# Two loads and two adds moved around the last groups of attention heads, and two transfers swapped in each pair's step

## The reference

```python
Q = Q * cos + _rotate_half(Q) * sin
K = K * cos + _rotate_half(K) * sin
scores = jnp.einsum('bhqd,bhkd->bhqk', Q, K) / scale
scores = jnp.where(causal, scores, jnp.float32(-jnp.inf))
attn = jax.nn.softmax(scores, axis=-1)
out = jnp.einsum('bhqk,bhkd->bhqd', attn, V)
out = out.transpose(0, 2, 1, 3).reshape(B, S, H)
return out @ Wo.T + bo
...
x = x + attention(layernorm(x))
x = x + (silu(xn @ gate_w.T * gate_s) * (xn @ up_w.T * up_s)) @ down_w.T * down_s   # xn = layernorm(x)
```

## Time and profile before

| what | value |
|---|---|
| median of 3 runs | 750.68 us (748.65 to 753.9) |
| the profiled execution | 749.88 us |
| its span, first to last instruction | 748.2 us |
| TensorE busy | 732.0 us, 98% |
| VectorE, ScalarE, GpSimd busy | 443.8, 310.9, 247.7 us |
| TensorE's granted clock | 0.999 |

### The profile page before, as it was taken

The page is one execution under the profiler, slowest core; times in us unless marked ns, Lnnn a source line. Parts: engine busy times, 40 slices in busy tenths (PEclk is TensorE's granted clock), DMA queues, the critical chain, the costliest instruction groups (busy, mean ns, idle before and its releaser), DMA issues.

```text
span 748.2 us, 10633 instructions
## 1 busy us (share of the span) xinstructions
PE 732.0 (98%) x3563; PEld 539.3 (72%) x3563; DVE 443.8 (59%) x1071; ACT 310.9 (42%) x641; POOL 247.7 (33%) x224
## 2 busy tenths in 40 slices
PE   8999999999999999999999999999999999999996
PEld 7887888766656666666666548788788888888885
DVE  6978684897778787777878545853243125114113
ACT  3322231266666666666666662222332232222221
POOL 0816152411114242333324245822232223223223
PEclk9999999999999999999999999999999999999999
DMA  8686469635576667676667356540001001001001
GB/s 280 230 284 232 162 254 309 255 115 160 162 192 172 185 172 194 168 188 164 187 162 187 102 185 225 222 201 1 0 20 38 0 1 56 0 0 56 1 1 59
DMA packets 54318, 104.39 MB, mean 140 GB/s; under 512 B 14820, under 2 KB 18404, under 8 KB 53748
## 3 DMA queue, kind: packets, MB, share of 16 engines
q1 hardware_dynamic: 54264, 103.72, 44.0%
HBM read 69.62 MB, written 38.21 MB: 144 GB/s over the span
## 4 chain that ended last, share of the span: by engine, by line
PE 81%; DVE 6%; issue 5%; DMA 3%; POOL 2%; ACT 1%; SPq 1%; DVEq 0%; POOLq 0%; ACTq 0%
PE ps L1105 32%; PE ps L1244 18%; PE ps L1130 10%; PE ps L1223 10%; PE ps L1320 9%; DMA x_st<-in_x 1%; PE ps L1097 1%; POOL hid_lo L592 1%; DVE xn L786 1%; DVE stats L771 1%; DMA rec_l<-rec_rows 1%; DMA w_st<-in_wk 1%; DMA l_cols<-o_raw 1%; ACT p L683 0%; DVE esin L893 0%
## 5 line engine op out<-in xcount | busy, mean ns | idle before, releaser
L683 ACT ACTIVATE p<-ps 128x384 f32<-128x384 f32 (+3 forms) x384 | 162.0, 489 | 58.0 <-PE ps L1223 57.8
L843 DVE CUSTOM_DVE_ANT_0 masked<-ps,mask_qk 128x512 bf16<-128x512 f32 (+1 forms) x240 | 113.2, 500 | 56.6 <-PE ps L1130 55.7
L1244 PE MATMUL ps<-p,v_slot 128*64 128x512 f32 (+3 forms) x768 | 137.3, 494 | 0.2 <-ACT o_raw L690 0.2
L1223 PE MATMUL ps<-q_st,k_st 99*128 99x384 f32 (+2 forms) x384 | 135.7, 361 | 1.1 <-ACT p L683 1.0
L1056 DVE SCALAR_TENSOR_TENSOR hid<-ps,us_sb,silu 128x512 f32<-128x512 f32 x44 | 33.0, 751 | 165.2 <-PE ps L1105 159.5
L1130 PE MATMUL ps<-k_st,q_st 96*128 96x512 f32 (+2 forms) x384 | 128.9, 357 | 2.0 <-DVE row_max L843 1.7
L592 POOL TENSOR_TENSOR hid_lo<-hid,hid_hi 128x512 fp32r<-128x512 f32 x44 | 56.8, 1290 | 173.0 <-ACT hid_hi L758 173.0
L561 POOL TENSOR_SCALAR_AFFINE_SELECT p<-p 128x512 f32<-128x512 f32 x64 | 40.6, 635 | 209.0 <-ACT p L683 209.0
L1244 PEld LDWEIGHTS ps<-p,v_slot 128*64 128x64 f32 x768 | 50.1, 136 | 74.2 <-issue 62.2
L1130 PEld LDWEIGHTS ps<-k_st,q_st 96*128 96x128 f32 x384 | 72.3, 189 | 29.7 <-DVE row_max L843 14.3
L1223 PEld LDWEIGHTS ps<-q_st,k_st 99*128 99x128 f32 x384 | 72.1, 189 | 16.9 <-issue 6.3
(11 more groups left out here) (117 smaller groups left out, 1080.8 us busy)
## 6 DMA issues: line engine op xcount, KB each, us to landing
qk_scratch<-st_hi SPq DMA_DIRECT2D x32, 512.0 KB, 3.6
q_st<-qk_scratch SPq DMA_DIRECT2D x32, 384.0 KB, 3.8
k_st<-qk_scratch SPq DMA_DIRECT2D x32, 384.0 KB, 4.8
flag_st<-in_ffn SPq DMA_DIRECT2D x32, 264.0 KB, 2.8
ffn_copy<-in_ffn SPq DMA_DIRECT2D x32, 264.0 KB, 3.5
qk_scratch<-st_lo SPq DMA_DIRECT2D x16, 512.0 KB, 3.7
o_T<-o_raw SPq DMA_DIRECT2D x32, 128.0 KB, 4.2
rec_l<-rec_rows SPq DMA_DIRECT2D x32, 128.0 KB, 3.3
```

The source lines that it names most:

```text
L683: act.activation(p32[:, at:at + q0 + w - keep], ps[:, ST_BANK + i % ST_RING, keep - q0:w], ACT.Exp, scale=SCALE).then_inc(exp_done, 1)
L843: ins = dve.tensor_tensor_reduce((masked_a if u < 2 else masked)[:, s_before(i) % 2, col:col + kept], scores, mask_qk[:, 512 - kept:512], ...
L1223: pe.matmul(ps[:, ST_BANK + i % ST_RING, 0:w], k_st[0:K_ALL, slot, kt * P:(kt + 1) * P], q_st[0:K_ALL, slot, q0:q0 + w], start=True, stop= ...
L1244: ins = pe.matmul(ps[VW * a:VW * (a + 1), o_bank(u, half), q0 - 512 * half:512], v_slot[:, slot, kt, :], p32[:, at:at + n], start=(kt == 0 ...
```

## The change

Two things move, and nothing is added or taken away.

In an even step SP's rows of maxima (`load_max(t + 1)`) now come ahead of `move_pair` and `store_rec`, and within `move_pair` the two moves of sums come ahead of the two moves of values.

At the end, the loads of `bo_sb` and `ds_sb` wait for one pair less of weighted values (`pv_half[1]` at 15 instead of 16) and come ahead of `move_pair(14)`; GpSimd does `add_bias(0)` ahead of `scale_group(6)` and `add_bias(1)` ahead of `scale_group(7)`.

```diff
--- before.py
+++ after.py
@@ -427,9 +427,11 @@
                     sp.wait_ge(l_out, 16 * (u // 2))
                 for a in range(2):
                     t = 2 * u + a
+                    sp.dma_start(l_cols[:, t % 4, :], o_raw[2 * D * a + D:2 * D * a + D + 1, u % 2, :].rearrange("o (p e) -> o p e", e=KT)).then_inc(o_moved[u % 2], 16)
+                for a in range(2):
+                    t = 2 * u + a
                     rows = slice(t % 4 * D, (t % 4 + 1) * D)
                     sp.dma_start(o_T[rows, t // 4, :], o_raw[2 * D * a:2 * D * a + D, u % 2, :]).then_inc(o_moved[u % 2], 16)
-                    sp.dma_start(l_cols[:, t % 4, :], o_raw[2 * D * a + D:2 * D * a + D + 1, u % 2, :].rearrange("o (p e) -> o p e", e=KT)).then_inc(o_moved[u % 2], 16)
 
             def store_rec(g):
 
@@ -445,12 +447,12 @@
                     sp.dma_start(rec_l[h * D:(h + 1) * D, :], rec_rows[g, h].partition_broadcast(D)).then_inc(rec_in, 16)
 
             def b_step(t):
+                if t + 1 < HEADS:
+                    load_max(t + 1)
                 if t % 2 == 0 and t >= 4:
                     move_pair((t - 4) // 2)
                 if t % 4 == 3 and t >= 7:
                     store_rec((t - 7) // 4)
-                if t + 1 < HEADS:
-                    load_max(t + 1)
 
                 cols = slice(t * FFN_PIECE, (t + 1) * FFN_PIECE)
                 if t == 0:
@@ -476,10 +478,10 @@
             sp.wait_ge(v_copied, HEADS)
             load_x(xr[:, 0, :, :], 0).then_inc(xr_in[0], 16)
             load_x(xr[:, 1, :, :], 1).then_inc(xr_in[1], 16)
-            move_pair(PAIRS - 2)
-            sp.wait_ge(pv_half[1], PAIRS)
+            sp.wait_ge(pv_half[1], PAIRS - 1)
             sp.dma_start(bo_sb[:, :], bo.partition_broadcast(P)).then_inc(c_in, 16)
             sp.dma_start(ds_sb[:, :], ds.partition_broadcast(P)).then_inc(c_in, 16)
+            move_pair(PAIRS - 2)
             move_pair(PAIRS - 1)
             store_rec(GROUPS - 1)
             load_rec(GROUPS - 1)
@@ -568,8 +570,6 @@
                 mask_p(t)
 
 
-            scale_group(GROUPS - 2)
-
             def add_bias(c):
                 pool.wait_ge(xr_in[c], 16)
                 for j in range(TJ):
@@ -578,8 +578,9 @@
 
             pool.wait_ge(c_in, 32)
             add_bias(0)
+            scale_group(GROUPS - 2)
+            add_bias(1)
             scale_group(GROUPS - 1)
-            add_bias(1)
             add_bias(2)
             add_bias(3)
```

## The result

The changed kernel takes 757.3 us (median of 18 executions, 752.97 to 761.93), the kernel before 750.03 us beside it (18 executions, 748.65 to 754.48). The ratio is 1.0085, 95% interval 1.0063 to 1.0108. It is slower by 0.85%. One execution of the kernel before in the second series, 910.2 us at a granted clock of 0.753, counts in no ratio. The forecast was 751.6 us in 748.6 to 756.0: the sign of the difference was right, the size was not, and 757.3 lies above the range.

The account below looks back on a forecast made before the run. The prediction took TensorE as the bound, busy 285.88 of 288.20 us in the heads stage, with one 1.2 us hole near 470. Adding +0.4 (steps) and +0.45 (hand-over), +0.9 on 750.68, gave 751.6 us, range 748.6 to 756.0.

Parts of the forecast that it names:

- Some 0.1 us: Even steps: the slack between VectorE's reciprocal and whole maximum and TensorE's transpose, put at some 0.1 us.
- rival 3: Steps: moves still land in 3.9 to 5.0 us, TensorE stalls at six transposes, 8 to 15 us slower; chance 0.10.
- Rival 2: Hand-over: late biases plus 1.9 us for shared operand reads make GpSimd the bound, +4 us, 755; chance 0.09.
- step 1: Heads' steps: the later moves make reciprocals slightly late; 0.4 us lost in all.
- 6 x 0 to 0.2 us: Even steps: six reciprocals wait for later moves, each costing TensorE 0 to 0.2 us; taken as 0.4 us in all.
- step 2: Hand-over to the output projection: GpSimd's chain ends at 470.2 and TensorE restarts 0.45 us later than before.
- +0.45: Hand-over: TensorE restarts at 471.9 against 471.46 in the profile before, 0.45 us later.
- The whole gain on offer is 1.2 us: Most to be gained by closing TensorE's hole near 470 us, plus at most 2.3 us in the stage before.
- S: Hand-over: time at which GpSimd can start its adds once the biases land; taken as 447.6, between 445.0 and 449.2 us.
- If they queue behind: Hand-over: bias loads land only after the `xr` loads, 446.5 plus 1.5 to 2.7 us, so adds start by 449.2.

Follow-up runs that it names:

- f0: The changed kernel, nothing altered, measured again beside the kernel before: ratio 1.0044, median 753.1 us.
- g4: The changed kernel, nothing altered, measured a third time beside the kernel before: ratio 1.0045, median 754.7 us.
- the part alone: Kernel before with only the steps' reordering (maxima ahead of moves, sums ahead of values), old hand-over, run twice: ratios 1.0019 and 1.0011.
- h2: Second run of the kernel before with only the steps' reordering, old hand-over: ratio 1.0011, median 751.6 us.
- f2: Changed kernel with VectorE's reciprocals put later, two pieces into the next step: ratio 1.0047 against the kernel before, median 754.1 us.
- g2: Changed kernel with VectorE's weight test three pieces sooner in even steps: ratio 1.0070 against the kernel before, median 757.6 us.
- e4: Kernel before with only the steps' reordering, and VectorE's reciprocals put two pieces into the next step: ratio 0.9990, median 749.9 us.
- c1: Kernel before with early bias loads and GpSimd's order group 6, adds of chunks 0 and 1, group 7; old steps: ratio 1.0000, median 750.8 us.
- g3: Kernel before with early bias loads, both adds between groups 6 and 7, and weight test three pieces sooner in even steps: ratio 0.9997, 751.1 us.
- g1: Kernel before with only VectorE's weight test three pieces sooner in even steps: ratio 1.0002, median 751.4 us.
- h3: Kernel before with only the maxima ahead of the moves, values still ahead of sums, old hand-over: ratio 1.0021, median 754.2 us.

## Why the prediction was right and wrong

**Held.** No gain in the steps, and nobody waits for the rows of maxima. "Some 0.1 us" of slack behind the reciprocal: measured 0.1 to 0.15. The moves 3.9 us later behind the maxima, their landing at 2.3 us (taken: 2.4), so rival 3 did not come. The late `xr` and bias loads: measured from the first output product, `xr` was forecast 12.17 us ahead of it and was issued 12.03, 12.21 and 12.16 us ahead (after, f0, g4), `bo_sb` 8.62 us ahead in forecast and 8.62, 8.63 and 8.63 in fact. GpSimd without a pause: 21.9 us for the four items against 22.6. The way from GpSimd's end to TensorE: 1.51 us against 1.55 to 1.95, so VectorE's residual add is no longer in the way. Rival 2 failed in its price: beside VectorE's splits group 6's multiply took 2.86 us and its add 3.17, together 0.8 us more than the 5.25 of the earlier trace rows, not 1.9.

**Failed, step 1: the steps' +0.4 us.** Measured the stage is 1.2 us longer (mean 292.9 against 291.7, four executions each), and the high-clock medians of the part alone 1.6 and 1.5 us. The sum had one term for it and set another to nothing.

The term for the reciprocals, "6 x 0 to 0.2 us", came out at 0.6 us, but not as written. It named a wait above 0.3 us as what would refute it, and the waits were 0.74 us once in the changed kernel, 0.39 in f0, 0.35 and 0.93 in g4, 0.15, 0.41 and 0.42 in h2, the others nothing. The median landing was right, but with a slack of 0.1 us the median is the wrong figure: landings of 3.2 us (step 18 of the changed kernel) and 3.3 us (g4's) go through.

The term put at nothing was the later `load_rec`: "GpSimd's `scale_group` and mask follow by that much, and the mask is wanted only a step later. I count 0". The mask was not what mattered. The multiply of `scale_group` holds up VectorE's weight test, and its later start made that test over 2 us long in two to four steps of each of the four profiles. That is 0.75 us of the 1.2. The prediction named this contention at the hand-over only.

**Failed, step 2: the hand-over's base.** "+0.45" was counted from a profile with a hole of 1.16 us, which was taken for the kernel's normal state. Counted like that the term was nearly right: the stage was 48.6, 47.7 and 47.2 us, mean 47.8, against 47.6 forecast. But six of eight executions with the old hand-over have no hole. Their stage is 45.7 to 45.9 us, the mean of all eight 46.1, so the edit costs 1.7 us. It took a hole that comes by chance, from one late piece of `rec_l`, and put one in its place that all three profiles have (1.2 to 2.5 us). "The whole gain on offer is 1.2 us" was 0 in six of eight.

**S**, the start of GpSimd's adds, came at 451.0, 449.7 and 448.5 us against 447.6. Relative to the first output product that is 1.8, 0.8 and 0.4 us later than forecast. I had let the biases half overtake the `xr` loads, since the `o_T` moves had the earlier trace rows. That reading was wrong for the second of these moves: issued at 441.35 with 2.87 us to landing, it landed at 444.22, no sooner than the load it was said to overtake (434.08 + 10.12 = 444.20). In the changed kernel neither did overtake: `ds_sb` landed 1.3 us behind the second `xr` load, and the `o_T` moves took 7.0 us instead of 2.7. "If they queue behind" was the right mechanism. S lies above its bound in the changed kernel, where the second `xr` load landed 0.04 us ahead of the first output product, and below it in f0 and g4, where it landed 2.0 and 2.2 us ahead. By the rule of the Trainium skill quoted in the prediction (DMA: Bandwidth & Descriptors, "Queues, rings and completion order") this was the expected end, and the trace agrees for `ds_sb`.

**Sum.** 1.2 and 1.7 us make 2.9, against the +0.9 of the forecast. That is 1.0039; the second and third series gave 1.0044 and 1.0045, the high-clock medians +2.1 and +2.2 us. Of the first series' 1.0085 it explains less than half, and with it alone the time would be near 753, inside the stated range. So it is the unexplained rest, 3.5 us by the ratio, that puts 757.3 above the range. In that series only 4 of 18 executions had a mean clock of 0.997 or more (median 753.4) and 7 lay below 0.994 (median 759.3), where f0 had 7 and 4 of 12 (752.1 and 757.1). The shares of the two groups alone move the median by several microseconds, and the prediction had no term for them. Why they differed in that series stays open: in the third the mean clock was as before's. That a hole of over 3 us is followed by a lower clock (f2, g2) is seen in two executions; that it happens more often with the change is only argued. The high-clock executions of the first series are also 1.3 us slower than those of the later two, and that stays open too.

No version tried beats the kernel before beyond its uncertainty: e4, c1 and g3 lie at 0.9990 to 1.0000.

## What to carry to other kernels

A hole in one profiled execution may be one late transfer: before an edit is costed by what it closes, look whether the landing time that makes it is the usual one or the maximum of its row, and count the same hole in a second execution. Where a step has 0.1 us of slack in front of the bounding engine, cost its move by the longest landing, not by the median. When a load comes later, ask what its user will now run beside, and not only who waits for the result. A run meant to test a cause must leave the rest in place: look whether the moved instruction stands ahead of something else. To find where a stage of equal steps has grown, compare the steps one by one. Loads brought forward behind 2 MB of others on the same queue do not come early; order the queue by who needs what first.

## What the runs showed of the hardware that was not expected

- Slow issues on SP come beside packets of the instruction queue. In step 18 the issue of a move took 1.1 to 1.6 us instead of 0.6 in ten of the eleven profiles with the late moves; in f0 it took 0.59, but landed in 2.8 us instead of 2.3. In all eleven a packet of that queue starts within 0.3 us of that issue's start. The changed kernel, 320 to 323 us (packets, MB, share of 16 engines):

```profile
q8 instruction: 1, 0.02, 2.4%
```

  Over all 18 profiles, 66 of 4941 issues between 152 and 440 us took over 1 us, and 59 of these start within 0.75 us behind such a packet's start or 0.2 us ahead of it; of all issues only 4% do. That the packet holds SP up is the likely reading, but no run moved it.
- Small loads behind large ones: `ds_sb` took 3.4 to 5.2 us behind small moves (eight profiles), 6.0 to 6.9 us when issued 5.8 us behind the last `xr` load (four), and 8.0 to 10.4 us when 3.3 to 3.5 us behind it (five).
- A VectorE instruction with two SBUF inputs beside GpSimd's multiply took up to 2.9 us instead of 0.69 (step 16 of g1), while the multiply kept its 2.4 us.
- Executions of one kernel fell in two groups (mean granted clock of 0.997 or more, and below 0.994), their medians 4 to 8 us apart. The profiled ones show stretches of 3.4 or 6.8 us at a granted clock of 0.5 (the 1.2 GHz level): near 170 us in five of 18, and behind the holes of 3.2 and 3.4 us at the hand-over. The window behind g2's hole:

```profile
478.00:482.00 4.00, 4.00 (x13) 3.09 (x12) 4.00 (x7) 0.00 (x0) 4.00 (x4) 0.57 0.00 0
```

Holes of 1.2 to 2.5 us (before, g4, h3, f0, after) had no such stretch behind them.
